# Counting-sort loop of a graph kernel: positions looked up from fp16 parts instead of fp32 tables

## The reference

```
h = relu(layernorm(x)); x = x + block0(h, edges)     # mean over neighbours, 3 layers, matmuls
h = relu(layernorm(x)); x = x + block1(h, edges)     # two attention heads
h = relu(layernorm(x)); x = x + block2(h, edges)     # 4 transformer layers, segment max and sum
h = relu(layernorm(x)); x = x + block3(h, edges, edge_attr)   # segment softmax, 4 heads
```

## Time and profile before

| | us |
|---|---|
| median of 3 runs | 13864.05 (13861.28 to 13869.13) |
| the profiled execution | 13865.12 |
| its span | 13863.3 |
| stage "rank" in it, from 332 to 1927 | 1595 |

### The profile page before, as it was taken

One profiled execution on the slowest core, in us unless ns is written; L12 is line 12 of the kernel. 1 busy time (PEld: TensorE's weight loads), 2 busy tenths in 40 slices (PEclk: granted clock), 3 DMA queues, 4 the chain that ended last, 5 costly groups with the idle time before them and its releaser, 6 DMA issues. The chain is left out here.

```text
span 13863.3 us, 184561 instructions
## 1 busy us (share of the span) xinstructions
PE 8195.2 (59%) x44926; PEld 6375.0 (46%) x44927; DVE 7917.9 (57%) x21423; ACT 6521.6 (47%) x14528; POOL 8822.9 (64%) x9142
## 2 busy tenths in 40 slices
PE   5888855555553111233466666666566656667887
PEld 4888842222221001233255535553555345545666
DVE  7666656655664222433367756765667657773555
ACT  7333333333333331466355536553555455534665
POOL 0555447777776776777577757775777577724664
PEclk9999997777775555565677787777777877775555
DMA  0000011121112112222444444443444444422223
GB/s 30 1 1 1 1 26 39 39 36 40 39 39 37 39 40 36 49 54 54 80 129 125 124 87 130 124 125 78 131 125 125 84 123 125 124 62 56 65 65 56
DMA packets 820853, 951.02 MB, mean 69 GB/s; under 512 B 482113, under 2 KB 557300, under 8 KB 820088
## 3 DMA queue, kind: packets, MB, share of 16 engines
q0 software_dynamic: 343040, 637.31, 20.1%
q1 hardware_dynamic: 475000, 299.57, 8.1%
q10 hardware_dynamic: 2304, 9.46, 0.2%
HBM read 859.25 MB, written 86.39 MB: 68 GB/s over the span
## 5 line engine op out<-in xcount | busy, mean ns | idle before, releaser
L1625 POOL DMA_INDIRECT work<-t,idx x3328 | 3174.9, 954 | 1221.0 <-issue 984.1
L769 POOL DMA_INDIRECT work<-t,idx x3328 | 3170.5, 953 | 1033.1 <-issue 1012.7
L781 ACT ACTIVATE work<-iota,loc 128x128 f32<-128x128 f32 (+1 forms) x6672 | 2034.4, 387 | 3528.1 <-DVEq L1075 1915.3
L1078 DVE TENSOR_TENSOR work<-work,ps 128x192 f32 x2496 | 882.2, 353 | 1226.9 <-PE ps L1102 926.4
L578 POOL DMA_INDIRECT tab<-work x784 | 806.4, 1029 | 1129.6 <-DVE work L438 660.1
L1102 PE MATMUL ps<-work 128*128 128x192 bf16 x2496 | 415.7, 306 | 1728.2 <-SPq L776 1664.6
L1719 PE MATMUL ps<-work 128*128 x6784 | 1296.2, 372 | 206.5 <-ACT work L794 170.3
L1719 PEld LDWEIGHTS ps<-work 128*128 128x128 f32 x6784 | 1282.7, 290 | 238.1 <-issue 219.4
L691 POOL DMA_INDIRECT tab<-work x784 | 831.9, 1061 | 716.2 <-POOLq L39 465.0
L1731 PE MATMUL ps<-work 128*128 128x136 f32 x6656 | 1272.9, 350 | 11.0 <-DVE work L1785 9.6
L2576 POOL DMA_INDIRECT work<-t,idx x832 | 790.1, 950 | 754.9 <-POOLq L2451 363.2
(11 more groups left out here) (399 smaller groups left out, 17483.5 us busy)
## 6 DMA issues: line engine op xcount, KB each, us to landing
work<-t,idx POOLq DMA_INDIRECT x7488
node<-pl SPq DMA_DIRECT2D x424, 256.0 KB, 3.4
work<-pl SPq DMA_DIRECT2D x54, 512.0 KB
work<-pl SPq DMA_DIRECT2D x106, 256.0 KB, 3.2
tab<-work POOLq DMA_INDIRECT x1568, 2.1
t<-work SPq DMA_DIRECT2D x196, 128.0 KB, 1.8
x<-work SPq DMA_DIRECT2D x196, 64.0 KB, 1.7
h<-work SPq DMA_DIRECT2D x28, 448.0 KB, 2.6
```

Of the source, the lines that this page charges most:

```text
L769: pool.indirect_dma_start(X[:, j % 4, n, :], None, table, bass.IndirectOffsetOnAxis(ap=idx[k][:, 8 * j + n:8 * j + n + 1], axis=0)).then_i ...
L781: t = act.activation(P[:, b, n, :], iota[:, :], ACT.Square, scale=-1.0, bias=loc[k][:, bass.ds(a + n, 1)])
L1078: added.on(dve.tensor_tensor(av, av, part(z, n), ALU.add))
L1625: pool.indirect_dma_start(X[:, j % 4, n, M - KD:W], None, table, bass.IndirectOffsetOnAxis(ap=idx[k][:, NT * j + n:NT * j + n + 1], axis=0 ...
```

## The change

The table R holds from now on only the counts of the present round of 16 columns (one iteration of the loop): it is cleared by a matmul with zeros at the first column of a round. `Rs` stays in SBUF as fp32 and holds the first positions less a constant (`MID`), brought up to date once a round on VectorE. `Bs` holds it as two fp16 parts, `Ds` the snapshot of R in fp16. A look-up is the sum of three fp16 matmuls (two in the first column of a round) in place of one fp32 matmul. The transposed one-hots are written as fp16, once, and `wide_half` is gone. `rows_of` adds `MID` back. The fourth `equal_high` moves behind column 7, and the fourth `column_pairs` behind the fourth `select`.

```diff
+            MID = float(64 * T)
...
-            OHhT, OHhTb = [None, None], [None, None]
+            OHhT = [None, None]
             for u in range(2):
-                OHhT[u], o = area(o, [HR, 2, 8, EP])
-                OHhTb[u], o = area(o, [HR, 2, 8, EP], BF)
+                OHhT[u], o = area(o, [HR, 2, 8, EP], HF)
             HT, o = area(o, [EP, 2, 16, EP], BF)
             triu, o = area(o, [EP, EP])
             junk, o = area(o, [EP, 4, 4 * LC])
-            Rs, o = area(o, [HR, 2, 2 * LC])
+            Rs, o = area(o, [HR, 2 * LC])
+            Bs, o = area(o, [HR, 2, 2 * LC], HF)
+            Ds, o = area(o, [HR, 2, 2 * LC], HF)
...
-                    pe.wait_ge(ldf.sem, ldf.up(2))
-                    pe.matmul(R, ident[0:HR, 0:HR], Rs[:, 0, :], start=True, stop=False, skip_group_check=True)
-                    for s in (tiles, cmpd, ldf):
+                    for s in (tiles, cmpd):
...
-                def select(dve, q, u):
-
-                    dve.wait_ge(found.sem, found.up())
+                def select(dve, q, u, wait=True):
+
+                    if wait:
+                        dve.wait_ge(found.sem, found.up())
...
+                def base(dve):
+
+                    v.on(dve.tensor_copy(Bs[:, 0, :], Rs))
+                    dve.wait_ge(v.sem, v.c)
+                    dve.tensor_tensor(Bs[:, 1, :], Rs, Bs[:, 0, :], ALU.subtract).then_inc(based.sem, 1)
+
                 def rows_of(dve, a, u):
+                    dve.wait_ge(v.sem, v.c)
+                    v.on(dve.tensor_scalar(POS[:, u, :], POS[:, u, :], MID, None, ALU.add))
...
+                    v.on(dve.tensor_scalar(Rs, Rs, -MID, None, ALU.add))
+                    dve.wait_ge(v.sem, v.c)
+                    base(dve)
...
                             column_pairs(dve, 1, 1 - u)
                             select(dve, 2, u)
                             column_pairs(dve, 2, 1 - u)
+                            dve.wait_ge(found.sem, found.up())
+                            if u:
+                                v.on(dve.tensor_tensor(Rs, Rs, R, ALU.add))
+                                dve.wait_ge(v.sem, v.c)
+                                base(dve)
+                            select(dve, 3, u, False)
                             column_pairs(dve, 3, 1 - u)
-                            select(dve, 3, u)
                             rows_of(dve, a, u)
...
                     for i in range(4):
-                        ht = OHhTb[u][:, i // 2, 2 * q + i % 2, :]
+                        ht = OHhT[u][:, i // 2, 2 * q + i % 2, :]
                         t = pe.matmul(HQ[:, i, :], ht, ht, start=True, stop=True)
...
-                    q = n // 2
-                    if n % 4 == 0:
-                        pe.wait_ge(turnedf.sem, turnedf.up(2))
-                    pe.wait_ge(snap.sem, snap.up())
+                    q, m = n // 2, 8 * u + n
+                    if m:
+                        pe.wait_ge(snap.sem, snap.up())
+                    else:
+                        pe.wait_ge(based.sem, based.up())
+                        pe.matmul(R, zer[:, 0:HR], zer[:, :], start=True, stop=False, skip_group_check=True)
                     for k in range(2):
                         t = count(pe, u, k, n)
-                    t.then_inc(counted.sem, 1)
+                    if m < 15:
+                        t.then_inc(counted.sem, 1)
                     if n % 2 == 0:
                         pe.wait_ge(ffree.sem, ffree.up())
                     for k in range(2):
-                        i = 2 * k + n % 2
-                        pe.matmul(LK[q][:, i, :], OHhT[u][:, k, n, :], Rs[:, n % 2, LC * k:LC * k + LC], start=True, stop=False)
+                        i, r = 2 * k + n % 2, slice(LC * k, LC * k + LC)
+                        ht = OHhT[u][:, k, n, :]
+                        pe.matmul(LK[q][:, i, :], ht, Bs[:, 0, r], start=True, stop=False)
+                        pe.matmul(LK[q][:, i, :], ht, Bs[:, 1, r], start=False, stop=False)
+                        if m:
+                            pe.matmul(LK[q][:, i, :], ht, Ds[:, m % 2, r], start=False, stop=False)
                         t = pe.matmul(LK[q][:, i, :], HT[:, u, 4 * q + i, :], OHl[:, 2 * k + u, n, :], start=False, stop=True)
...
+                                if 3 <= n < 6:
                                     equal_high(pe, n - 3, 1 - u)
+                            equal_high(pe, 3, 1 - u)
...
-                    own.on(act.copy(OHhTb[u][:, k, r, :], BT[k][:, r, :]))
-                    act.wait_ge(own.sem, own.c)
-                    act.sem_inc(turned.sem, 1)
-
-                def wide_half(act, k, h, u):
-
-                    r = slice(4 * h, 4 * h + 4)
-                    act.copy(OHhT[u][:, k, r, :], OHhTb[u][:, k, r, :]).then_inc(turnedf.sem, 1)
+                    act.copy(OHhT[u][:, k, r, :], BT[k][:, r, :]).then_inc(turned.sem, 1)
...
                             for n in range(8):
-                                act.wait_ge(counted.sem, counted.up())
-                                act.copy(Rs[:, (n + 1) % 2, :], R).then_inc(snap.sem, 1)
-                                if n == 0:
-                                    wide_half(act, 1, 1, u)
-                                elif n < 5:
+                                m = 8 * u + n
+                                if m < 15:
+                                    act.wait_ge(counted.sem, counted.up())
+                                    act.copy(Ds[:, (m + 1) % 2, :], R).then_inc(snap.sem, 1)
+                                if 1 <= n < 5:
                                     turned_half(act, (n - 1) % 2, (n - 1) // 2, 1 - u)
-                                else:
-                                    wide_half(act, (n - 5) % 2, (n - 5) // 2, 1 - u)
```

More of the change, by code:

```diff
@@ L304, in _ @@
                 def _(act):
-                    act.copy(Rs[:, 0, :], R).then_inc(counted.sem, 1)
+                    act.copy(Rs, R).then_inc(counted.sem, 1)
                 @block.sync
@@ L311, in _ @@
                         sp.dma_start(counts[k].rearrange("(h l) -> h l", l=LC),
-                                     Rs[:, 0, LC * k:LC * k + LC]).then_inc(put.sem, 16)
+                                     Rs[:, LC * k:LC * k + LC]).then_inc(put.sem, 16)
                     sp.wait_ge(put.sem, put.up(2))
@@ L320, in _ @@
                     for k in range(2):
-                        sp.dma_start(Rs[:, 0, LC * k:LC * k + LC],
+                        sp.dma_start(Rs[:, LC * k:LC * k + LC],
                                      firsts[k].rearrange("(h l) -> h l", l=LC)).then_inc(ldf.sem, 16)
-                    for s in (counted, put, first, put2):
+                    sp.wait_ge(ldf.sem, ldf.up(2))
+                    for s in (counted, put, first, put2, ldf):
                         s.back(sp)
@@ L385, in group_edges @@
                 sig = signals(nc, st, "rank")
-                high, low, tr, turned, turnedf = sig("high"), sig("low"), sig("tr"), sig("turned"), sig("turnedf")
+                high, low, tr, turned, based = (sig("high"), sig("low"), sig("tr"), sig("turned"), sig("based"))
                 heq, htd, counted, snap = sig("heq"), sig("htd"), sig("counted"), sig("snap")
@@ L447, in _ @@
                     heq.back(dve)
+                    v.back(dve)
                     with dve.Fori(0, ET // 16) as i:
@@ L503, in _ @@
                 def _(pe):
-                    waited = (high, low, turned, turnedf, htd, snap, ffree)
-                    pe.sem_inc(snap.sem, 1)
+                    waited = (high, low, turned, based, htd, snap, ffree)
                     pe.sem_inc(ffree.sem, 4)
@@ L520, in _ @@
                                     turn(pe, n, 1 - u)
-                                if 3 <= n < 7:
+                                if 3 <= n < 6:
                                     equal_high(pe, n - 3, 1 - u)
+                            equal_high(pe, 3, 1 - u)
                         for s in waited:
@@ L526, in _ @@
                     pe.wait_ge(htd.sem, htd.up())
-                    pe.wait_ge(turnedf.sem, turnedf.up(3))
-                    pe.wait_ge(snap.sem, snap.up())
+                    pe.wait_ge(based.sem, based.up())
                     pe.wait_ge(ffree.sem, ffree.up(4))
@@ L552, in _ @@
                         turned_half(act, k, h, 0)
-                    for k, h in ((0, 0), (1, 0), (0, 1)):
-                        wide_half(act, k, h, 0)
-                    for s in (tr, own):
-                        s.back(act)
+                    tr.back(act)
                     with act.Fori(0, ET // 16):
@@ L559, in _ @@
                             for n in range(8):
-                                act.wait_ge(counted.sem, counted.up())
-                                act.copy(Rs[:, (n + 1) % 2, :], R).then_inc(snap.sem, 1)
-                                if n == 0:
-                                    wide_half(act, 1, 1, u)
-                                elif n < 5:
```

(6 more changed lines are left out.)

## The result

| us | before | changed |
|---|---|---|
| median | 13865.81 (13861.28 to 13869.13) | 13543.88 (13540.37 to 13552.14) |
| span of the profiled execution | 13863.3 | 13538.5 |

The ratio is 0.9769, 95% interval 0.9752 to 0.9786. 324.8 us of span are gone where 235 were forecast. The runs of one kernel spread by 8 and 12 us.

The account below looks back on a forecast made before the run. The rank stage was taken to be bound by a ring of TensorE and VectorE. A round falls from 32.6 to 27.8 us, 49 x 4.8 = 235 us, so 13865 - 235 = 13630 us, range 13585 to 13715.

Parts of the forecast that it names:

- The ring: Rank loop: TensorE from turn 0 to column 7, then VectorE to the next turn 0; a round 27.8 us, before 32.6.
- 16-bit look-up, pace p: TensorE in a column: each 16-bit matmul (98x128 weights, 64 columns) takes 0.06 us, so a column takes 0.64.
- base: VectorE between column 7 and select 3, once a round: add, fp16 copy, subtraction and two waits, 0.95 us on the ring.
- half without / with base: Rank loop, turn 0 to turn 0: 13.1 us, and 14.7 in the half that adds the base and 0.65 idle.
- MID's step: VectorE between select 3 and turn 0: one added dependent small operation, 0.2 us.
- The clock: TensorE in the rank stage already runs at 1.2 GHz, can't fall further, and all prices are for that level.
- Behind the loop: The 11936 us behind the rank stage run the same code on the same data and enter the sum at nothing.
- GpSimd against the base: Rival: the base's fp16 copy waits for one scatter's 0.96 us once a round, 47 us, total 13677; chance 0.09.
- The snapshot slower than 0.72: Rival: snapshots between directly following columns take 1.1 us a pair as ScalarE is busy, 69 us, total 13700; chance 0.07.
- Weights set the pace: Rival: weight loads make look-ups 0.10 to 0.107 us, a column 1.0, total 13800; chance 0.05.
- Sums in one place wait for each other: Rival: matmuls adding to the same PSUM columns wait for one another, stage 600 us longer, total 14460; chance 0.04.
- The clock rises: Rival: the denser stream lifts TensorE to 2.4 GHz, VectorE becomes the bound, half a ring about 11.5 us, total 13475; chance 0.05.

Follow-up runs that it names:

- h4: Changed kernel, scatters left out, plus four extra ScalarE copies of 98x512 fp32 a half, each waited for; mean half 13.632 us.
- h1: Changed kernel, scatters left out, with the old order (equal_high 3 before column 7, pairs 3 before select 3); halves 14.66 us with the base, 13.20 without.
- h5: Kernel before, scatters left out, plus eight extra zero-weight matmuls of 512 16-bit columns behind column 0; mean half 13.655 us in place of 16.296.
- i1: Changed kernel, scatters kept, plus six extra 256-column matmuls behind equal_high 3 and eight behind column 0; 13483.59 us, ratio 0.9724 to the kernel before.
- g2: Changed kernel with the rank loop's scatters left out; mean half 13.166 us, 13.153 with scatters.
- g3: Kernel before, scatters left out, plus eight extra matmuls of 256 16-bit columns behind column 0; mean half 16.084 us, seven halves of 13.8 to 13.9.
- g4: Changed kernel, scatters left out, plus four extra 256-column matmuls behind equal_high 3 and four behind column 0; mean half 13.308 us.
- e, f and h runs: Variants of both kernels, h without scatters, on chips where the kernel before takes 19283.01 (e), 19289.17 (f) and 18683.39 us (h).
- g1: Kernel before with the rank loop's scatters left out; mean half 16.296 us, halves of 15.95 and 16.65 as with scatters.
- e4: Kernel before with only the new order of equal_high 3, column 7, select 3 and pairs 3; 19232.68 us, ratio 0.9979 on a slow chip.

## Why the prediction was right, and where it was wrong

**The ring: right.** Each step can be laid beside the low-clock halves.

| step | forecast | measured |
|---|---|---|
| 16-bit look-up, pace p | 0.06 (0.053 to 0.08) | 0.053 |
| count to count, columns 2 and 3 | 0.72 | 0.69 (603.48 to 604.17) |
| base | 0.95 (0.7 to 1.3) | 0.79 |
| select 3, from turn 0 | 9.03 | 8.88 |
| select 3 to turn 0 | 4.08 | 3.99 |
| half without / with base | 13.1 / 14.7 | 12.86 / 14.32 |

Nearly every term was priced a little high. Together that is 27.8 - 27.2 = 0.6 a round, 49 x 0.6 = 29 us: with the right sizes the forecast would have been 13600, within the range. MID's step (0.2) was as forecast, and h4 puts the wide copies at 0.06 a half where the forecast had nothing. The old order costs 0.34 a half, as h1 shows.

**The clock: the step that failed.** "So it can't fall further, and all prices above are already for that level." The first half of the sentence is true, the second isn't: the level rose. Half by half at the low clock the loop would be about 98 x 13.59 = 1332 us, and it is 98 x 13.153 = 1289: 43 us that the sum had at nothing. It is the largest of the terms that were missed. The sum with the clock's 43 alone put right is 13587, just inside the range, and with all but the clock put right 13583, just outside: no single term explains the miss.

The rival that said so had a chance of 0.05, for two reasons that the runs correct. It argued from "at 85% busy" in the kernel before. But between 707.90 and 721.87 that kernel's TensorE is idle for 0.11 us in all and stays at the low pace, while the changed kernel is less busy (64%) and has the risen clock. So the busy share of the records did not decide the level here. The look-ups, fp32 in one and fp16 in the other, are the largest difference between the two, and h5's fill of bf16 matmuls brought the high clock to the old loop; but h5 also takes idle time away, and no run changed the kind of the look-ups alone. That fp32 kept the clock down fits all traces and is not shown. And the rival was made all or nothing (13475), with nothing in between; in truth the clock rises in 66 of the 93 halves, and for part of each.

**Behind the loop: 15.8 us that I had at nothing.** Same code, same data, but not the same time. Half of one block shows where (groups by line, GpSimd, 3400 us of the trace of the changed kernel and, in the second fence, the same work before):

```profile
L1640 POOL DMA_INDIRECT work<-t,idx x1953 | 1865.3, 955 | 686.1 <-issue 582.2 <-DVEq L1869 90.9 <-POOLq L2195 13.1
```

```profile
L1625 POOL DMA_INDIRECT work<-t,idx x1953 | 1863.4, 954 | 707.4 <-issue 579.2 <-DVEq L1854 115.1 <-POOLq L2180 13.1
```

The gathers are equal in number and length; the waits for VectorE's queue are 24 us shorter. i1 has 93.6 there. Why, I did not test; this stays open. It is one trace of each kernel, and their runs spread by 8 and 12 us, so part of it may be that spread.

The sum of the 324.8: ring as forecast 235, over-priced terms 29, clock 43, behind the loop 16, the ends of the loop 2.

**The rivals.**
- GpSimd against the base: out. The copy took 0.226 to 0.229 us in all 49 rounds, each time with a scatter running for part of it at least, and 0.226 to 0.228 in g2 without any. GpSimd still waits 2.2 to 3.5 us between halves. Nothing here shows the lock-out that the Trainium skill (SBUF — State Buffer, Who interferes with whom) describes for such a copy.
- The snapshot slower than 0.72: out, it was 0.69.
- Weights set the pace: out. By the Trainium skill (TensorE: Matmul & The Clock Gate, LDWEIGHTS) 128 columns of weights would take an estimated 107 ns; the look-ups start 53 ns apart, and 30 ns apart at the high clock.
- Sums in one place wait for each other: out, by the same 53 ns.
- The clock rises: right in kind, and worth 43 us of the 155 that it was priced at. i1 shows 54 more of them. Its price for a half was right too: 11.5, and the shortest halves of i1 take 11.32, at a clock of 0.81 to 1.00. In one of them (from 433.59) VectorE is busy for 9.80 us and waits for TensorE for 0.67 only, so it is the bound there, as the rival had it.

**Open.** What exactly decides in which halves the clock rises; in g3 it rises 160 or 225 us apart, in regular turn, so not at random. Why g4's smaller fill lowered it and h4 kept it down. What the scatters do on the chips of the e, f and h runs. Running rows_of behind the first one-hot, which would take it off the ring, wasn't tried.

## What to carry to other kernels

Rebuild the ring from the rows, part by part: here it gave the halves at one clock to 2 or 3%, and its parts could be tested at their own price. But price it at both clock levels, and give the level a chance that is not all or nothing. Where TensorE runs at 0.50 in a latency-bound loop and idles before a wait that it can't shorten, try cheap 16-bit matmuls in the idle time, in more than one size: fourteen a half gained 60 us here, eight lost 0.14 us a half. Compare variants half by half at one clock, since in h4 an edit worth 0.06 us a half came with 0.47 through the clock.

## What the hardware showed that I had not expected

- The loop with fp32 look-ups kept TensorE 85% busy for 1.6 ms at the pace of 1.2 GHz. With 3.3 us of bf16 matmuls with zero weights in the idle time of each half (h5), the granted clock was 0.75 on average, and the fp32 look-ups behind them took 0.25 in place of 0.46.
- The page prints 1.00 for a stretch in which the pace is the low one (g1 too: 16.296 a half, printed 1.00). The first change of clock on record in the trace of the kernel before lies at 2040 us. Ahead of it the printed number is not a measurement; a known matmul's pace is.
- One kernel took 13.87 ms on some chips and 18.68 or 19.28 on others, and 2% changes of the ring don't show there at all. In the rank loop the difference goes with the scatters (h1 to h5 leave them out and don't have it). That is no rule for all indirect DMAs: a stretch of 174 us with 100 of them (from 5462 in the kernel before, from 6543 in e4) is equally long on both kinds of chip.
- In the changed kernel's loop most scatters take 0.96 us. All 145 of the 784 that take 1.18 us or more run beside one-hots of VectorE (and 97 shorter ones do too), while the one-hots are as long as in g2 without scatters. It looks as if GpSimd is the one held up; no run tests it.
